# Moving DMA loads from the SyncE queue to the GpSimd queue in an attention and feed-forward layer

## What is computed

```python
xn = _layernorm(x)                       # x: (2, 8192, 2048) f32
q = rope((xn @ Wq + bq))                 # 16 heads of 128
k = rope((xn @ Wk + bk)); v = xn @ Wv + bv   # 4 kv heads
scores = einsum('bhtd,bhTd->bhtT', q, k) / sqrt(128)
attn = softmax(scores + causal_bias) @ v
attn = attn @ Wo + bo
ffn = qlinear(silu(qlinear(xn, gate)) * qlinear(xn, up), down)   # 8-bit weights, 5632 hidden
out = x + attn + ffn
```

## Time and profile before

| what | us |
|---|---|
| median of the two runs shown | 8058.2 |
| the two runs | 7888.47 and 8227.92 |
| the profiled execution, its time | 7862.96 |
| its span, the slowest core | 7861.4 |
| the other cores' spans | 7835.2 to 7860.5 |
| TensorE busy in the span | 4925.8 (63%) |
| VectorE busy | 2297.9 (29%) |
| ScalarE busy | 1914.1 (24%) |
| GpSimd busy | 215.3 (3%) |

### The profile page before, as it was taken

One profiled execution on the slowest core, in us unless ns is written; L12 is line 12 of the kernel. 1 busy time (PEld: TensorE's weight loads), 2 busy tenths in 40 slices (PEclk: granted clock), 3 DMA queues, 4 the chain that ended last, 5 costly groups with the idle time before them and its releaser, 6 DMA issues.

```text
span 7861.4 us, 82452 instructions; the slowest of 8 cores (7835.2 to 7861.4 us)
## 1 busy us (share of the span) xinstructions
PE 4925.8 (63%) x29504; PEld 2494.5 (32%) x29504; DVE 2297.9 (29%) x4914; ACT 1914.1 (24%) x2851; POOL 215.3 (3%) x380
## 2 busy tenths in 40 slices
PE   2444444445888889788888844467774446677555
PEld 1122211222333347533335731133442113344322
DVE  3554455453111112211112213331111333211133
ACT  0111111111111100011110001157774115677500
POOL 0000000000000000000000000000000000000000
PEclk9666666667888899888889967778897777889788
DMA  2111111111000001200001130000003000000155
GB/s 89 63 62 48 53 63 56 51 57 59 25 25 24 26 29 54 68 25 24 25 25 36 53 127 22 11 9 5 5 4 100 22 11 1 1 1 1 54 171 145
DMA packets 147692, 339.59 MB, mean 43 GB/s; under 512 B 18400, under 2 KB 57440, under 8 KB 137568
## 3 DMA queue, kind: packets, MB, share of 16 engines
q1 hardware_dynamic: 124896, 260.76, 11.0%
q0 software_dynamic: 22400, 73.56, 2.5%
HBM read 271.26 MB, written 62.98 MB: 43 GB/s over the span
## 4 chain that ended last, share of the span: by engine, by line
PE 50%; DVE 20%; ACT 13%; DMA 8%; issue 8%; DVEq 1%; ACTq 0%; SPq 0%; POOL 0%; POOLq 0%
PE P L259 44%; ACT ptb L239 9%; PE P L253 6%; DMA out<-ost 2%; DVE s1c L239 2%; DMA wqf<-wq 2%; DMA wof<-wo 1%; DMA ff_scr<-dst 1%; DVE P L239 1%; DVE wgbx L239 1%; DVE xnT L239 1%; DVE wubx L239 1%; DVE xnb L239 1%; DVE attb L239 1%; ACT fgo L239 1%
## 5 line engine op out<-in xcount | busy, mean ns | idle before, releaser
L239 ACT ACTIVATE ptb<-P,ccol 128x1024 bf16<-128x1024 f32 (+3 forms) x1664 | 1293.8, 816 | 561.2 <-PE P L253 340.8
L259 PE MATMUL P<-xnf,wgbx 128*128 128x512 bf16 x2816 | 808.1, 452 | 361.8 <-DVE wubx L239 361.8
L259 PE MATMUL P<-vh,ptb 128*128 128x129 bf16 x7424 | 662.9, 227 | 435.6 <-ACT ptb L239 421.9
L259 PEld LDWEIGHTS P<-vh,ptb 128*128 128x128 bf16 x7424 | 467.9, 100 | 960.2 <-issue 958.9
L259 PE MATMUL P<-wdbx,guT 128*128 128x257 bf16 x5344 | 667.6, 283 | 73.1 <-DVE dst L239 68.2
L239 DVE TENSOR_TENSOR P<-P,masks_s 128x128 f32<-128x128 f32 x1024 | 254.8, 295 | 1371.1 <-PE P L253 1369.8
L259 PE MATMUL P<-xnf,wubx 128*128 128x512 bf16 x2816 | 638.4, 380 | 0.0
L259 PEld LDWEIGHTS P<-wdbx,guT 128*128 128x128 bf16 x5344 | 535.7, 101 | 172.2 <-issue 91.2
L239 DVE TENSOR_TENSOR guT<-fgo,fgo 128x512 bf16<-128x512 f32 x176 | 121.9, 692 | 1580.2 <-ACT fgo L239 1580.2
L259 PE MATMUL P<-ident_bf,xnb 128*128 128x128 bf16 x768 | 119.2, 301 | 718.0 <-DVE xnb L239 683.0
L259 PEld LDWEIGHTS P<-xnf,wgbx 128*128 128x128 bf16 x2816 | 303.2, 112 | 826.4 <-issue 634.0
(11 more groups left out here) (121 smaller groups left out, 4401.0 us busy)
## 6 DMA issues: line engine op xcount, KB each, us to landing
xb<-x_full SPq DMA_DIRECT2D x64, 1024.0 KB, 4.8
wg<-wg SPq DMA_DIRECT2D x88, 256.0 KB, 2.7
wu<-wu SPq DMA_DIRECT2D x88, 256.0 KB, 3.0
wd<-wd SPq DMA_DIRECT2D x176, 128.0 KB, 2.1
ff_scr<-dst POOLq DMA_DIRECT2D x128, 128.0 KB, 2.2
wqf<-wq SPq DMA_DIRECT2D x32, 512.0 KB, 4.8
xnq<-xo_scr SPq DMA_DIRECT2D x8, 2048.0 KB, 7.7
wof<-wo SPq DMA_DIRECT2D x64, 256.0 KB, 3.3
```

The costliest lines, as they stand in the source:

```text
L239: getattr(e, m)(*aa, **kk).then_inc(s.h, 1))
L259: e.matmul(out=o, lhsT=l, rhs=r, start=st, stop=sp, skip_group_check=sk))
```

## The change

In each attention half the load of the first `xnq` chunk is issued first on SyncE, right after the barrier, instead of behind the sixteen Wq tiles. The rope tables (half 0) and both `kth` loads go from SyncE to GpSimd, in the order rope tables, kth, vh, kth, vh. `kth` now counts on vh's semaphore, and the rope tables keep theirs. In the output projection the `xo4` and `yf4` loads, and the wait for `ring_free` before them, go from SyncE to GpSimd, where they stand ahead of the block's store in the text.

```diff
         for H in range(2):
             barrier()
+            if H == 0:
+                dma("gpsimd", qKV, qrope[:, 0:OWN], qcos_in[:, :])
+                dma("gpsimd", qKV, qrope[:, OWN:2 * OWN], qsin_in[:, :])
+            rope_cnt = qKV.cnt
+            ldxq0 = dma("sync", qXQ, xnq3[:, :, :], xo_pv[:, :, 0:512])
             for gl in range(2):
-                dma("sync", qKV, kth[:, gl * T:(gl + 1) * T], kt_scr[2 * H + gl][:, :])
+                dma("gpsimd", qKVg, kth[:, gl * T:(gl + 1) * T],
+                    kt_scr[2 * H + gl][:, :])
                 dma("gpsimd", qKVg, vh[:, gl * 8256:(gl + 1) * 8256],
                     v_scr[2 * H + gl][:, :])
-            if H == 0:
-                dma("sync", qKV, qrope[:, 0:OWN], qcos_in[:, :])
-                dma("sync", qKV, qrope[:, OWN:2 * OWN], qsin_in[:, :])
-            kv_cnt, kvg_cnt = qKV.cnt, qKVg.cnt
+            kvg_cnt = qKVg.cnt
...
             for qch in range(4):
-                wait("sync", sPE, qmm_last)
-                ldxq = dma("sync", qXQ, xnq3[:, :, :],
-                           xo_pv[:, :, qch * 512:(qch + 1) * 512])
+                if qch == 0:
+                    ldxq = ldxq0
+                else:
+                    wait("sync", sPE, qmm_last)
+                    ldxq = dma("sync", qXQ, xnq3[:, :, :],
+                               xo_pv[:, :, qch * 512:(qch + 1) * 512])
...
-                        wait("vector", qKV, kv_cnt)
+                        wait("vector", qKV, rope_cnt)
...
-            wait("tensor", qKV, kv_cnt)
...
             for tt in range(16):
-                wait("sync", sV, ring_free[tt % 2])
-                dma("sync", qXY[tt % 2], xo4[tt % 2][:],
+                wait("gpsimd", sV, ring_free[tt % 2])
+                dma("gpsimd", qXY[tt % 2], xo4[tt % 2][:],
                     x_own[tt * 128:(tt + 1) * 128, dc * 512:(dc + 1) * 512])
-                ldy = dma("sync", qXY[tt % 2], yf4[tt % 2][:],
+                ldy = dma("gpsimd", qXY[tt % 2], yf4[tt % 2][:],
                           ff_scr[tt][:, dc * 512:(dc + 1) * 512])
```

## The result

The changed kernel takes 1.0293 times the time of the kernel before, 95% interval 1.0233 to 1.0353; the median of its runs is 8175.2 us (11 runs, 8118.3 to 8350.2), that of before 7948.3 us (10 runs). The profiled execution took 8141.6 us, spans 8072.9 to 8140.1 us over the cores.

A forecast was written before the change was run, and what follows sets the result against it. The projection was taken as bound by the store's loop over two buffers, 4.0 us a block, not by matmuls. Projection +216 and entries -20 gave +196 us on 7863.0, said as 8060 us; range 7990 to 8230.

The forecast's parts named there:

- The loop 3.79 + L: Projection, one block: store issue, two more issues, yf's landing, VectorE's start and adds; 8.0 us, +216 us over sixty steps.
- L: Projection: yf's landing time when GpSimd issues it, taken as 4.2 us; 3.3 would give +162, 5.1 would give +270.
- the clock fell: Projection: TensorE's granted clock may drop from 1.00 toward 0.50, hidden by under 14 us of cover: 0 us.
- SyncE's freedom: Projection: SyncE has only wof and may run ahead, but stops at two tiles: 0 us.
- -20 us: Both attention entries together: gain from xnq going first and kth and rope tables moving to GpSimd, between -37 and -10.
- The low end: Entries: GpSimd's share passes first and the wq stream moves back by xnq; 3 and 7 us less, sum -10.
- equal shares: Entries, upper end: GpSimd's and SyncE's transfers share the DMA engines by equal bytes; 20 and 17 us less, sum -37.
- The base of the steps: Projection: the 60 steps between blocks before the change, 263.6 us in all, which 480 us would replace.
- Sum: Whole kernel: +216 - 20 = +196 us on the profiled execution's 7863.0 us, said as 8060 us, 2.5% more.
- Short loads: Rival, projection: yf lands in under 3.55 us, no loss beyond 2%; with 3.3, +142, 8005 us; chance 0.23.
- The move does not bind: Rival, projection: GpSimd's loads precede the adds, steps stay 4.4 us; entries' gain leaves 7825 to 7853 us; chance 0.02.
- Long loads: Rival, projection: yf lands in 5.1 to 5.7 us, +270 to +306, less 10: 8123 to 8159 us; chance 0.20.

The follow-up runs named there:

- the two middle experiments: Changed kernel with loads one block earlier on GpSimd: ratio 0.9999; kernel before with SyncE's loads also waiting for block tt-1's adds: ratio 1.0234.
- all changes together: Kernel before plus late kth and vh, half 1's wq during half 0, projection loads on SyncE in rings of four, Wo casts within steps: ratio 0.9704.

## Why the prediction was right and wrong

**The mechanism, step by step.** "The loads of tt+1 can't go before the adds of tt": as forecast; it is what the two middle experiments separate. The loop 3.79 + L: on core 6 yf's landing, all 64 loads, is

```profile
DMA to landing us min/median/max: 3.9/4.2/14.4
```

and the steps are 498.8 / 60 = 8.3 us. L was taken as 4.2, and the median is 4.2; the landings on the chain that ended last have a mean of 4.37 on this core (3.9 to 6.2; the 14.4 is not on the path), since they are skewed to the long side and each of them is now on the path. A median was used where a sum over all steps wants the mean. The 3.79 was short as well: from yf's landing to the first add 0.16 us pass in the chain (7527.45 + 4.12 to 7531.73), where 0.05 was taken; rows 4, for a store, already have 0.09. Both together are 60 x (0.17 + 0.11), 17 us too little. The store was gone from the waits, the clock fell and cost nothing in the loop, and SyncE's freedom gained nothing; all as said. (By the fit of the Trainium skill, DMA: Bandwidth & Descriptors, Anatomy of one DMA, an estimate for such a transfer is 2.6 us. The store, now issued first of three, has a median of 2.7 on this core, so it agrees there; for yf, issued third in a row, it is 1.6 too short.)

**The entries.** -20 us was taken between ends of -37 and -10; measured was -13.6 on core 6 and -9.6 in the mean. The low end was the right picture: GpSimd's large packets passed first, and the wq stream moved back by xnq. The row on packet sizes spoke for it, and I still went half-way to equal shares. Against the mechanism that is 6 to 10 us.

**The base of the steps.** 263.6 us was core 6's own, with 77.7 in the last group. The other cores had 239.9 to 257.1. Only core 7 had a last group like it (74.1), and in the changed kernel the last group is no longer than the others, so a base with that group in it was too high for what comes after: the sum over steps rose by 235 us on core 6 but by 247 in the mean. The gaps' +7.8 us on core 6 was not in the sum either; over the cores it is +2.6. With the mean cores' base (15 us), the longer loop (16) and the smaller gain of the entries (10), +196 becomes +237; the mean of the eight spans rose by 242.5 us, from 7850.6 to 8093.1.

**The sum and the time.** +196 us was forecast, 2.5% of the profiled execution; the span of core 6 rose by 232.7, the ratio by 2.9%. Direction and size of the change held: 8060 / 7863.0 = 1.025 lies in the measured interval. The step that failed is the last one, the paragraph **Sum**. 8060 us was set on the profiled execution and printed beside a median of 8058.2 us, against which it says that nothing changes. The ratio on that median is 8058.2 x 1.0293 = 8294 us, above the upper end of 8230. Two runs 340 us apart could not say which level the kernel's time would be quoted at, and the range allowed for half of that spread where the whole would have been needed. Ten runs put the median of before at 7948.3 us; at this level the forecast would have been 8147, near the 8175.2 measured.

**The rivals.** "Short loads" needed L under 3.55; in the projection's loop no yf of any core landed under 3.6. "The move does not bind" did not happen. "Long loads", L of 5.1 and more, did not come either: the slowest, core 4, has 515.0 us in 60 steps, 8.6 a step, with a median landing of 4.5.

## What to carry to other kernels

Before moving a DMA to another engine, write out that engine's list and find the wait that it will stand behind: the same loads on the same queue cost 2.9% behind the wait for the block's adds, and one entry earlier nothing that an interval of 0.6% would show. A loop that a landing time divided by the number of buffers sets is mended with more buffers (-0.9% here), not with another queue. The gain lasts only as long as the engine that then bounds keeps its clock: all changes together had TensorE at 0.81 and steps of 4.2 us on half of the cores. When a wait moves onto the path of every step, price it with the mean of its landings, on a core whose rows are like the others'.

## What was not expected of the hardware

Two queues did not share the DMA engines by bytes or one packet for one: with GpSimd's packets at 12.1 KB and SyncE's at 1.0 KB, 77.5% to 17.4% of the engines' time, and with rows of 2 KB on GpSimd's side (3.3 KB a packet) 54.2% to 38.6%. In both, two packets or a little more of SyncE's passed for one of GpSimd's. What sets that number is open, and so is how much of the second pair is due to the smaller DMAs rather than to the rows.

In the changed kernel's profiled execution cores 4 and 5 needed 8 to 12 us more in each half's attention than the other cores' mean, in code that the change leaves alone. Their xnq loads were slower, here core 4's eight against 7.5 in the median on core 6:

```profile
  DMA xnq<-xo_scr: 13.4, 6
...
DMA to landing us min/median/max: 10.0/10.3/40.8
```

The first line is TensorE's idle time until an xnq had landed: three times in each half, 6.7 us a half. No core of before (medians of 7.3 to 8.3 us) and no other core of this execution shows it; its cause stays open.
